# Fourteen weight pieces per head group, split two a step in seven steps

## The reference

```python
q = (hidden_states @ Wq.T).reshape(B, L, H, D)      # rotary embedding on q and k
k = (hidden_states @ Wk.T).reshape(B, L, KVH, D)
v = (hidden_states @ Wv.T).reshape(B, L, KVH, D)
...
scores = jnp.einsum('bhnid,bhnjd->bhnij', qc, kc)
y_intra = jnp.einsum('bhnij,bhnjd->bhnid', scores * decay, xc)
k_dec = kc * jnp.exp(Glast - G)[..., None]
cstates = jnp.einsum('bhnjd,bhnje->bhnde', k_dec, xc)
_, prev = lax.scan(step, init, (...))               # state * dec + cs
y_inter = jnp.einsum('bhnid,bhnde->bhnie', qc * jnp.exp(G)[..., None], prev)
...
y = y / rms * gnorm_w
gate = (hidden_states @ Wg.T).reshape(B, L, H, D)
y = y * (gate * jax.nn.sigmoid(gate))
return y.reshape(B, L, H * D) @ Wo.T
```

## Time and profile before

| | |
|---|---|
| median of 3 executions | 1928.74 us (1928.62 to 1933.93) |
| the profiled execution | 1936.2 us, of which its span (first to last instruction) 1934.4 us |
| PE busy | 1735.3 us, 90% of the span |
| DVE, POOL, ACT busy | 1404.4 us (73%), 1225.3 us (63%), 1141.4 us (59%) |
| mean granted TensorE clock | 0.939 of 2.4 GHz |
| weight pieces loaded and split | 112, each 256 KB, 2.7 us median from issue to landing |
| `WL` on POOL, on DVE | 75 and 37 |

### The profile page before, as it was taken

The page is one execution under the profiler, slowest core; times in us unless marked ns, Lnnn a source line. Parts: engine busy times, 40 slices in busy tenths (PEclk is TensorE's granted clock), DMA queues, the critical chain, the costliest instruction groups (busy, mean ns, idle before and its releaser), DMA issues.

```text
span 1934.4 us, 39417 instructions
## 1 busy us (share of the span) xinstructions
PE 1735.3 (90%) x11652; PEld 978.2 (51%) x11652; DVE 1404.4 (73%) x3143; ACT 1141.4 (59%) x3012; POOL 1225.3 (63%) x1153
## 2 busy tenths in 40 slices
PE   5668998989989898989989898989989998999976
PEld 4534454545545454545545454545545454555544
DVE  6976676768867677667767677768867677678875
ACT  5446565656656565656756565656656565656642
POOL 1236676666767576657767676666767576666633
PEclk8779999989999899989999899989999899999997
DMA  4111102010111102010111102010111002100002
GB/s 163 33 34 34 34 18 71 29 41 23 34 61 34 30 17 72 28 41 21 36 57 33 35 17 72 28 41 23 34 61 35 29 17 72 28 29 23 23 1 88
DMA packets 38536, 77.29 MB, mean 40 GB/s; under 512 B 4768, under 2 KB 5792, under 8 KB 37152
## 3 DMA queue, kind: packets, MB, share of 16 engines
q1 hardware_dynamic: 38304, 74.47, 12.3%
HBM read 69.99 MB, written 4.46 MB: 38 GB/s over the span
## 4 chain that ended last, share of the span: by engine, by line
PE 60%; POOL 18%; issue 11%; DVE 4%; ACT 4%; DMA 2%; POOLq 0%; ACTq 0%; DVEq 0%; SPq 0%
PE B L298 18%; PE B L299 18%; PE B L300 18%; POOL QS L1099 4%; POOL WL L1093 3%; PE B L781 2%; POOL WVL L1130 2%; POOL WVF L1122 2%; POOL ROWS L1112 2%; DMA STAGE<-in_wall 2%; POOL RR L1141 2%; POOL QL L1104 1%; ACT XN L417 1%; POOL RM L1138 1%; PE B L447 1%
## 5 line engine op out<-in xcount | busy, mean ns | idle before, releaser
L1134 POOL TENSOR_TENSOR PL<-PF,PH 128x512 bf16<-128x512 f32 x128 | 155.7, 1216 | 390.6 <-ACT PH L934 390.6
L298 PE MATMUL B<-XTH,WH 128*128 128x512 bf16 x640 | 250.5, 391 | 52.8 <-DVE QF L1261 52.1
L934 ACT ACTIVATE PH<-PF 128x512 bf16<-128x512 f32 x128 | 80.5, 629 | 360.2 <-DVE PF L1295 360.2
L298 PE MATMUL B<-WH,XTH 128*128 128x512 bf16 (+1 forms) x1024 | 288.1, 305 | 3.2 <-POOL WL L1093 3.2
L299 PE MATMUL B<-WL,XTH 128*128 128x512 bf16 (+1 forms) x1024 | 286.8, 304 | 0.0
L300 PE MATMUL B<-WH,XTL 128*128 128x512 bf16 (+1 forms) x1024 | 286.3, 304 | 0.0
L299 PE MATMUL B<-XTL,WH 128*128 128x512 bf16 x640 | 250.1, 391 | 0.0
L300 PE MATMUL B<-XTH,WL 128*128 128x512 bf16 x640 | 248.8, 389 | 0.0
L1295 DVE SCALAR_TENSOR_TENSOR PF<-B,DT,PF 128x128 f32<-128x128 f32 x512 | 143.5, 341 | 138.1 <-PE B L300 132.4
L1099 POOL TENSOR_TENSOR QS<-QS,SIN 128x512 f32<-128x512 f32 x160 | 206.1, 1288 | 41.5 <-ACT QS L890 39.9
L298 PE MATMUL B<-WH,ZTH 128*128 128x512 bf16 x512 | 197.4, 386 | 36.5 <-POOL WL L1093 36.5
(11 more groups left out here) (158 smaller groups left out, 4494.6 us busy)
## 6 DMA issues: line engine op xcount, KB each, us to landing
ROWS<-rows_dram SPq DMA_DIRECT2D x128, 256.0 KB, 3.1
STAGE<-in_wall SPq DMA_DIRECT2D x112, 256.0 KB, 2.7
ACC<-in_x SPq DMA_DIRECT2D x4, 1024.0 KB, 7.8
out<-ACC SPq DMA_DIRECT2D x3, 1024.0 KB, 3.9
COS<-in_cos SPq DMA_DIRECT2D x1, 1024.0 KB, 12.8
SIN<-in_sin SPq DMA_DIRECT2D x1, 1024.0 KB, 14.5
out<-ACC SPq DMA_DIRECT2D x4, 256.0 KB, 2.5
EBF<-in_eb SPq DMA_DIRECT2D x1, 256.0 KB, 4.3
```

Source lines behind the costliest of these rows:

```text
L298: nc.tensor.matmul(out_, ah, bh, start=first, stop=False)
L1134: nc.gpsimd.tensor_tensor(PL[:, n % 2, :], PF[:, :], PH[:, n % 2, :], ALU.subtract).then_inc(pl_ready.sem, 1)
```

## The change

The 14 pieces are split two a step, in steps 9 to 13, 17 and 18, each pair one on POOL and one on DVE (before, 9 of 14 were on POOL). Pieces are loaded a step ahead of their split (12 and 13 now at 17). ACT splits ahead of slot B and of the decay; in step 18 ahead of `square`. POOL and DVE split at the very end of their step; in step 18 ahead of the mask of the rows, and behind `zt_lo`. At step 14 PE waits for the gate's `WL` pieces one by one, each just ahead of the three matmuls that read it, and no longer for all four ahead of the first.

```diff
--- before.py
+++ after.py
@@ -50,10 +50,10 @@
 AFTER_FILL = {0: 3, 1: 2, 3: 2, 5: 2, 7: 3, 8: 2}
 AFTER_FILL_PEELED = {0: 3, 1: 3, 2: 3, 3: 2, 4: 4, 5: 2, 6: 4, 7: 3}
 
-HI = {9: (0,), 10: (1, 2), 11: (3, 4, 5), 12: (6, 7, 8), 13: (9,), 17: (10, 11), 18: (12, 13)}
-LO_POOL = {9: (0,), 10: (1,), 11: (3, 5), 12: (6, 7), 13: (9,), 17: (10,), 18: (12,)}
-LO_DVE = {10: (2,), 11: (4,), 12: (8,), 17: (11,), 18: (13,)}
-LOADS = {3: (0, 1), 9: (2,), 10: (3, 4), 11: (5, 6, 7), 12: (8, 9), 13: (10, 11), 18: (12, 13)}
+HI = {9: (0, 1), 10: (2, 3), 11: (4, 5), 12: (6, 7), 13: (8, 9), 17: (10, 11), 18: (12, 13)}
+LO_POOL = {n: HI[n][:1] for n in HI}
+LO_DVE = {n: HI[n][1:] for n in HI}
+LOADS = {3: (0, 1), 9: (2, 3), 10: (4, 5), 11: (6, 7), 12: (8, 9), 13: (10, 11), 17: (12, 13)}
 POOL_LO = [i for n in sorted(LO_POOL) for i in LO_POOL[n]]
 DVE_LO = [i for n in sorted(LO_DVE) for i in LO_DVE[n]]
 
@@ -699,8 +699,8 @@
                 if fresh:
                     piece = item if item <= PV_ else PG + KT - 1
                     pe.wait_ge(wh_ready.sem, wh_ready.at(gw, piece))
-                    for i in range(PG, PG + KT) if item == PG else (piece,):
-                        signal, k = wl_of(i)
+                    if item <= PV_:
+                        signal, k = wl_of(piece)
                         pe.wait_ge(signal.sem, signal.at(gw, k))
                 if item < PV_:
                     for k in range(KT):
@@ -716,6 +716,9 @@
                 else:
                     t = t0 + (item - PG) * P
                     for k in range(KT):
+                        if fresh and item == PG:
+                            signal, i = wl_of(PG + k)
+                            pe.wait_ge(signal.sem, signal.at(gw, i))
                         ins = mm3(out_bank[:, :], XTH[:, k, t:t + P], XTL[:, k, t:t + P], WH[:, PG + k, :], WL[:, PG + k, :],
                                   k == 0, k == KT - 1)
                 ins.then_inc(ring_full.sem, 1)
@@ -1041,8 +1044,12 @@
                     wv_hi(g, n + 1)
                 if n == 0:
                     act.wait_ge(d_sent.sem, 16 * NB)
+                if n % NCH == 2:
+                    next_weights()
                 square(g, n)
                 state_hi(g, n)
+                if n % NCH != 2:
+                    next_weights()
                 if s >= 2 and now:
                     slot("B")
                 if s == 0 and now:
@@ -1055,7 +1062,6 @@
                 if s == 1 and now:
                     slot("B")
                     hi(g, b + 1, now["A"])
-                next_weights()
                 if s == 1 and now:
                     slot("C")
                 if s == 2 and now:
@@ -1173,6 +1179,10 @@
 
                 def sine(x):
                     times_sin(g, b + 1, now[x])
+
+                def next_lo():
+                    for i in weights_at(LO_POOL, n, last):
+                        split_lo(g + 1 if n >= PEEL else g, i)
                 if nxt:
                     p_lo(g, n + 1)
                     weighted_v(g, n + 1)
@@ -1182,6 +1192,8 @@
                     lo(g, b + 1, FILLS[1]["A"])
                 if s < 2 and now:
                     sine("A")
+                if n % NCH == 2:
+                    next_lo()
                 if not (last and n >= NCH - 2):
                     mask_rows(g, n + 2)
                 inv_rms(g, n)
@@ -1193,10 +1205,10 @@
                     lo(g, b + 1, FILLS[1]["B"])
                 if s == 1 and now:
                     sine("B")
-                for i in weights_at(LO_POOL, n, last):
-                    split_lo(g + 1 if n >= PEEL else g, i)
                 if s == 0 and now:
                     sine("C")
+                if n % NCH != 2:
+                    next_lo()
 
             for n in range(PEEL):
                 step(0, n, False)
@@ -1389,6 +1401,10 @@
                     else:
                         silu2(g, b + 1, now[x] - PG, use(now[x]))
 
+                def next_lo():
+                    for i in weights_at(LO_DVE, n, last):
+                        w_lo(g + 1 if n >= PEEL else g, i)
+
                 def add(item):
                     add_sin(g, b + 1, item, use(item))
                 if nxt:
@@ -1421,13 +1439,13 @@
                     add_out(g, n - 2, last)
                 if s == 1 and now:
                     q_lo(g, b + 1, FILLS[0]["C"])
-                for i in weights_at(LO_DVE, n, last):
-                    w_lo(g + 1 if n >= PEEL else g, i)
                 if now:
                     slot("B")
                 if s == 0 and now:
                     add(now["B"])
                     slot("C")
+                if n % NCH != 2:
+                    next_lo()
 
             for n in range(PEEL):
                 step(0, n, False)
```

## The result

The changed kernel takes **1834.1 us** (median of 4 executions, 1832.84 to 1835.38) where the kernel before, on the same chip, takes 1930.84 (1928.62 to 1933.93): a ratio of 0.950, 95% interval 0.948 to 0.952. The profiled execution took 1833.69 us, 102.5 less than that of before.

A forecast was written before the change was run, and what follows sets the result against it. PE, busy 90%, was taken to lose time in two stretches per group: steps 12 and 13, and step 2. Terms -65.4 + 8.1 + 11.3 - 46.5 = -92.5 gave 1836 us from the median; range 1812 to 1862, about 0.85.

The forecast's parts named there:

- step 13: Both `STAGE` waits go, item 1's bank is free in time, PE full at 13.53 us a step: -65.4 us.
- step 10: DVE's added `WL` makes `PF` and the last `QL` late; scores wait 1.1 to 1.2 us, seven times: +8.1 us.
- step 14: Same delay as step 10 plus 0.85 us inherited from ACT's pair; step takes 13.75 us: +11.3 us.
- steps 2 and 3: Over eight groups, from 262.97 to 216.5 us, the 4.56 us wait for piece 12 gone: -46.5 us.
- Step 2: PE's wait for piece 12 goes; last `QL` ends at +14.1, so PE waits 2.3 us for the scores.
- The loop: On six of eight passages PE jumps back; scores start 5.17 us after the last release, at +14.6.
- The clock: Each gap before step 3 costs 1.6 us at half rate, making it 12.45 us; gaps of about 1.2 cost nothing.
- dear small waits: Rival, 0.12: fourteen 1.1 to 1.5 us waits before steps 11 and 15 also drop the clock: +22, 1858 us.
- More than forecast: Rival, 0.14: no clock loss behind 2.3 to 2.7 us gaps and no inherited delay in step 14: 1817 us.
- Step 13 is not cured: Rival, 0.06: item 3's or 6's fill still waits 3 us and loses the clock: +32, 1868 us.
- slower: Rival, 0.03: DVE's `WL` ahead of `PF` also waits, delaying the last `QL` at steps 10, 14, 18: 1929 us and above.

The follow-up runs named there:

- the last two experiments: Changed kernel with DVE's `WL` ahead of the output gating in every second step of a block: 1823.6 us; that plus POOL's second `QL` directly behind the first: 1815.0 us.
- tables-only kernel: Kernel before with the new piece and load tables, old places in the step and old gate wait: 1936.9 us, ratio 0.9996.
- early-`QL` kernel: Changed kernel with POOL's second `QL` moved directly behind the first: 1822.8 us, ratio 0.942.
- both moves: Changed kernel with POOL's second `QL` directly behind the first and DVE's `WL` ahead of the output gating in every second step of a block: 1815.0 us, ratio 0.937.
- no early place: Changed kernel with pieces 12 and 13 split at the same place as in other steps, not early in step 18: 1869.8 us, ratio 0.965.
- wait for all four: Changed kernel with PE's old single wait for all four gate `WL` pieces ahead of the first gate matmul: 1853.1 us, ratio 0.958.
- DVE's `WL` early: Changed kernel with DVE's `WL` ahead of the output gating in every second step of a block: 1823.6 us, ratio 0.942.

## Why the prediction was right, step by step

It said 1836 and named each place. By the same windows the terms come to:

| term | forecast | measured |
|---|---|---|
| step 13 | -65.4 | -65.4 |
| step 10 | +8.1 | +9.5 |
| step 14 | +11.3 | 0.0 |
| steps 2 and 3 | -46.5 | -44.1 |
| sum | -92.5 | -100.0 |

The other 2.5 us between the profiled executions lie outside these steps: attention starts 2.6 later (157.89 for 155.33), step 13 of the last group takes 1.7 more, and the part behind the last scores takes 6.9 less (81.92 for 88.85), with PE busy 54.7 us there instead of 62.2 at an unchanged order. No term had that, and the other kernels speak against its being the change's. The part behind the last scores takes 89.7 and 88.7 us in the last two experiments, which contain the change, and 81.9 to 89.7 in all eight kernels. The attention starts between 155.3 and 156.5 in the other seven, and step 13 of the last group takes 8.3 in six of them. What sets these stays open.

*Step 13.* Right: 13.53 in every group, ACT's waits gone. The tables-only kernel shows that the spread alone leaves it at 15.46. The rest came with the new places, DVE's `WL` behind slots B and C and ACT's pair ahead of slot B; the two were not tested apart.

*Step 10, new.* The mechanism held: `PF` at +2.10 and `QL` at +12.84, forecast 2.10 and 12.85. The size was short by 0.2 a step, because I read the 0.24 between the end of `QL` and the scores as slack. After the change, with PE idle and waiting, it is 911.38 - 911.15 = 0.23 again: so much passes between POOL's end and these scores. It is not the same everywhere: at the end of the last group's step 2 it is 0.09, and matmuls that waited for POOL's `WL` started 0.05 to 0.15 us after it. The early-`QL` kernel shows that PE was ready at 11.50; in the kernel before, `QL` had already held it by 0.22. The Trainium skill (SBUF — State Buffer, "Who interferes with whom") has the two `WL` exclude each other, and here the trace agrees: DVE's, issued at 899.45, ended at 900.49, 0.55 after POOL's.

*Step 14, likewise.* This is the step that failed. I gave it the chain of step 10, with `WVF` and `WVL`. But POOL makes no weighted values for a group's last chunk (120 `WVF` in 128 steps): the windows show 8 POOL instructions there against 11 in step 10, and even the earlier trace rows had it, with 7.31 us of POOL work in step 14 and 10.07 in step 10. The inherited delay did come, and in the size forecast: `PF` starts at +2.98 in step 14 and at +2.10 in step 10, 0.88 later for 0.85. But the chain behind it is two instructions shorter, so `QL` ends at +11.66, not +13.7, and the scores start at +12.13, as before: no new wait in front of step 15, and the term is 0.0 us for 11.3. The same term passed over the one-by-one wait, which is worth 23 us in this step: without it two pieces ending in step 14 would have cost more than my 11.3.

*Step 2* and *The loop.* The scores start at +14.76 for 14.6 forecast, but for another reason. I let the jump decide (last release + 5.17) with `QL` inside at 14.1. `QL` ends at +14.53 and decides: the last group, which does not jump, has nearly the same, 14.64. It is 0.4 late because `ROWS`, beside DVE's `WL` of piece 13, took 1.72 us (1.26 in other steps). And 5.17 was too long. With `QL` out of the way, the scores came 4.2 to 4.5 us after the last `WL` in the kernel with both moves (4.46 from 994.90 to 999.36) and 4.2 to 4.9 after it with `QL` early alone; by these the jump would have let the scores go at +13.6 to +14.3, ahead of `QL`. Counting from the last release fits the runs, though: in the second of these kernels it comes 0.86 us later than in the first (+10.23 for +9.37), and the scores come 0.9 us later in the mean. In the kernel before, where PE had stood 4.6 us for that release and ran at a low clock behind it, it was 5.0 to 5.6.

*The clock.* Step 3 averages 12.50 us, forecast 12.45, by luck in part: it runs from 11.64 to 13.80 behind gaps of the same 3.1 us. That the 1.41 us waits leave the clock alone was right, and with it the rival of dear small waits fell: step 11 keeps 10.85 at clock 1.00.

*More than forecast* happened in half, and for another reason than it gave: the inherited delay came in step 14 but cost nothing, and the clock loss was there. *Step 13 is not cured* and *slower* did not happen.

## What to carry to other kernels

When a piece of background work is spread over steps, what counts is which waiting instruction it stands in front of: the same tables gave nothing at the old places and 5% with new ones and a split wait (the new places with the old tables were not run). Before adding a delay to a chain in another step, count that step's own instructions in a window; and check with an edit whether a small distance between a release and its user is slack or always there. A wait for several things in front of a run of matmuls should be split, each just ahead of its reader.

## What the runs showed of the hardware

The jump of the hardware loop cost PE 2.0 to 2.4 us per pass in the kernel with both moves (13.55 to 13.89 against 11.52) and 2.8 to 3.5 with `QL` early alone (14.42 to 15.14 against 11.60), where the last `WL` that PE waits for in front of it is ready 0.86 us later. DVE stood 2.77 us at the same place in the first of them. The Trainium skill (Advanced Engine Details and Errata, "Control Flow Timing") gives some 0.1 us for a compare-and-branch; the trace shows much more around it, and doesn't show what fills the time.

The length of a gap did not decide the clock alone. These are gaps of PE in front of the scores, and whether some of the next step's matmuls ran at the 1.2 GHz level:

| kernel, step | gap, us | clock fell |
|---|---|---|
| changed, no early place, wait for all four; step 11 | 1.40 to 1.46 | 0 of 21 |
| both moves; step 3 | 1.9 to 2.2 | 1 of 6 |
| only the tables; step 11 | 2.33 | 5 of 7 |
| DVE's `WL` early; step 3 | 2.5 to 3.3 | 8 of 8 |
| `QL` early; step 3 | 2.7 to 3.4 | 4 of 6 |
| changed; step 3 | 3.0 to 3.5 | 7 of 8 |
| wait for all four; step 3 | 3.0 to 3.5 | 4 of 8 |

The steps 2 of the last two kernels are the same to 0.03 us. What else decides stays open.
